# Cross-attention stage of a pre-norm decoder layer: two of four exponential tiles transposed by DMA, and row sums taken from the value product

## Chip, cores and metric

One Trainium2 chip, one core. The metric is the device time of one execution in microseconds (us), median of three runs.

## What is computed

```python
x = x + self_attention(layernorm(x))     # x: 4 rows x 2048 tokens x 512, f32
x = x + cross_attention(layernorm(x), ctx, ctx, mask)   # ctx: 4 x 128 x 512, 16 heads of 32
x = x + ffn(layernorm(x))                # s = x @ Win (64 wide); h = relu(s*W1+b1), 16 per channel;
                                         # g = sum(h*W2)+b2; out = g @ Wout
# cross attention, per head: p = exp(q.k/sqrt(32) - max); out = (p @ v) / sum(p)
```

The self-attention stage works on other axes and fills the first 848 us of the span. The change lies in the second stage, which does the cross attention and the FFN together.

## The kernel before

**Steps and slots.** The second stage goes through 8192 tokens in 16 steps j of 512 tokens, each of four tiles t of 128 tokens. Every engine has its own program order, written out by hand in its `step(j, p)`: the four slots t = 0 to 3, and then a tail. On TensorE a slot begins with `scores(t)` (q times k of all 16 heads of tile t, into four PSUM banks `sc`). The other work of a slot belongs to tiles further down the pipeline, and `ffn_out(0)` opens the step. The tail is `ffn_in(j-1)`, `norm2_T(3)`, four `queries(m)` (the q of the next step) and `prob_T(14)`, `prob_T(15)`.

**A tile's softmax.** DVE takes the maxima (`tops(t, g)`, g = four heads), ACT the exponentials (`exps(t, g)`: four instructions of 128x128, each with `accum_out`, which gives the row sum to `total`). TensorE transposes the exponentials, four heads to a PSUM bank (`prob_T(i)`, i = 4t + g, 16 a step). ACT copies each bank to f16 (`prob_hi`, into `pT[0]`), and DVE subtracts that copy from the bank (`prob_lo`, into `pT[1]`), so that high and low f16 part carry the value together. `values(t)` (48 matmuls of 128x32: 16 heads by three products of high and low parts) multiplies the tile before by v. `normalise(t)` on DVE divides by the sums, `attn_T(t)` transposes, `attn_hi`/`attn_lo` split again, and `out_proj(t)` multiplies by Wo; its split low part comes from `attn_lo(t)`. `add_attn(t)` adds the residual, `statistics(t)` takes mean and variance, and POOL's `norm2` makes the normalised tile that `norm2_T(t)`, `norm2_hi/lo` bring to `ffn_in`.

**The FFN tail.** After `ffn_in`, ACT and DVE work in turns on eight `hinges` (ACT a relu, DVE a multiply-add into `g_sb`), mixed with the splitting of q; then ACT's `gate_hi` and DVE's `gate_lo` give `gT`, which the next step's `ffn_out(0)` waits for.

**POOL** does the first normalisation (`norm(i)`), the residual plus bias (`residual(i)`) and `norm2`; the last `norm2` of a step is `norm2(j + 1, 0)`. **SP** issues all DMAs from one queue in program order: the load of the next x (`x1`), the stores, `load_ctx` (k, mask, v).

**The ring.** All PSUM results but the scores go round four banks. A hand-written order `TURNS` gives each a place; `bank(j, turn)` waits until the user four places before has been read (`taken`).

**Waits that matter below.** `scores(t)` waits for the last exponentials of the tile before, since it overwrites their banks. `exps(t, g)` waits for the transposes of the tile before, since there is one buffer `prob`.

Of the kernel before, what the change touches and what calls it, by code (L numbers as in the profile page):

```python
# [21 lines left out]
F32 = mybir.dt.float32  # L22
# [25 lines left out]
PASSES = ((0, 0), (0, 1), (1, 0))  # L48

# [54 lines left out]
def first_block(nc, x_in, ctx_in, mask_in, x1_dram, st_dram, w_in, b_in, scratch, keep):  # L104

    with ExitStack() as stack:
# [19 lines left out]
        with ExitStack() as early:  # L126
# [10 lines left out]
            vparts = sb0("vparts", [P, R, 2, D], F16)  # L137
# [11 lines left out]
        aT = [[sb(f"aT{b}_{h}", [P, DK, P], F32R) for h in range(2)] for b in range(2)]  # L149
        x = [keep["x_tile"], sb("x_tile1", [P, R, D])]  # L150
# [19 lines left out]
        total = sb("total", [P, R, H])  # L170
# [33 lines left out]
        v_trans, v_h, v_l = sem("v_trans"), sem("v_h"), sem("v_l")  # L204
        k_prod, k_masked, k_hi, k_lo = sem("k_prod"), sem("k_masked"), sem("k_hi"), sem("k_lo")
# [45 lines left out]
        def _(sp):  # L251
# [10 lines left out]
            def store_ctx():  # L262
# [366 lines left out]
        def _(act):  # L629
            def step(j, p):  # L630
# [206 lines left out]
        def _(dve):  # L837
# [334 lines left out]
def slot_turns(t):  # L1172
# [17 lines left out]
    "pT": lambda j, i: 16 * j + i + 1,  # L1190
# [23 lines left out]
def tile_at(t, lag, parity):  # L1214
# [5 lines left out]
ENDING = [(END, "pT", 14), (END, "pT", 15), (TILES, "aT", 0), (END, "x2T", 3), (TILES, "pv", 0), (TILES, "wo", 0),  # L1220
# [3 lines left out]
        if active(j, kind, i) and (j, kind, i) not in ENDING] + ENDING  # L1224
PLACE = {turn: n for n, turn in enumerate(RING)}
# [12 lines left out]
def bank_before(j, turn):  # L1238

    at = PLACE[(j, *turn)] - 4  # L1240
    if at < 0:
        return None
    step, kind, i = RING[at]
    return kind, TURNS_OVER[kind](step, i)


CROSS_SMALL = [("kt", [P, 2, DK, C], F32R), ("fillrows", [P, C], F32R), ("v_c", [C, 2, 2, D], F16),
# [4 lines left out]
def load_rows(sp, row, scratch, ahead, k_in, v_in, p):  # L1252
# [5 lines left out]
    sp.dma_start(ahead["v_c"][:, p, :, :],  # L1258
                 scratch["v"].rearrange("r c a n -> (r c) a n")[row * P:(row + 1) * P, :, :]).then_inc(v_in[p], 16)
# [13 lines left out]
def cross_block(nc, x1_dram, st_dram, scratch, w_in, b_in, out, keep):  # L1273

    with ExitStack() as stack:
# [12 lines left out]
        sb("bout_place", [P, D])  # L1288
        for name, shape, dt in CROSS_SMALL:
# [10 lines left out]
        pT = [sb(f"pT{h}", [C, H, P], F16) for h in range(2)]  # L1300
        attn = sb("attn_c", [P, D])
        aT = [sb(f"aT_c{h}", [P, DK, P], F32R) for h in range(2)]
# [3 lines left out]
        g_sb = sb("g_sb", [P, 4 * P])  # L1306
        gT = [sb(f"gT{h}", [P, 4 * P], F32R) for h in range(2)]
        ntop = sb("ntop", [P, H])
        total = sb("total_c", [P, 2, H])
        rtotal = sb("rtotal", [P, H])  # L1310
# [5 lines left out]
        ring = [stack.enter_context(nc.psum_tensor(f"ring{i}", [P, 512], F32)) for i in range(4)]  # L1316
# [5 lines left out]
        consts, k_zero = sem("c_consts"), sem("k_zero")  # L1322
# [3 lines left out]
        bn2_done, mv2_done, var2_done, rstd2_done, x2m_done, xn2_done, bf_added = (  # L1326
            sem(f"c_{n}") for n in ("bn2", "mv2", "var2", "rstd2", "x2m", "xn2", "bf_added"))
        scored, topped, exped, summed = sem("scored"), sem("topped"), sem("exped"), sem("summed")
        relu_done, hinged, g_hi, g_lo = sem("relu_done"), sem("hinged"), sem("g_hi"), sem("g_lo")
# [8 lines left out]
        def _(sp):  # L1338
# [19 lines left out]

            def step(j, p):
# [20 lines left out]
            store(TILES + 1, 1, 3)  # L1380
# [5 lines left out]
        def _(pool):  # L1386
            def step(j, p):
# [10 lines left out]
                def residual(i, j=j):  # L1398

                    wait(pool, taken["wo"], 4 * (j - 1) + i + 1)  # L1400
                    nc.gpsimd.tensor_tensor(xr[(j + 1) % 2][:, i, :], x1[:, i, :], bo[:, :], ALU.add).then_inc(res_done, 1)

# [49 lines left out]
        def _(pe):  # L1452
            def bank(j, turn):

                before = bank_before(j, turn)
                if before:
                    wait(pe, taken[before[0]], before[1])
# [14 lines left out]
            def step(j, p):  # L1472
# [40 lines left out]
                def ffn_out(t, j=j):  # L1513
                    if not active(j, "out", t):
                        return
                    cols = slice(t * P, (t + 1) * P)
# [531 lines left out]
```

## Time and profile before

| | us |
|---|---|
| median of three runs (1783.1 to 1784.54) | 1783.86 |
| the profiled execution's own time | 1784.44 |
| its span in the profile | 1782.6 |
| mean granted TensorE clock | 0.983 |
| PE, DVE, ACT, POOL busy, share of the span | 95%, 85%, 60%, 57% |
| one step in the steady state (1186.77 to 1243.76 us) | 56.99 |

PE is TensorE's matmuls, PEld its weight loads, DVE VectorE, ACT ScalarE, POOL GpSimd. Instructions of one engine overlap somewhat: the distance from one start to the next is what an instruction takes of its engine, and its own duration is a little longer.

### The profile page before, as it was taken

What the parts mean: (1) busy time and instruction counts of PE and PEld (TensorE: products, weight loads), DVE (VectorE), ACT (ScalarE), POOL (GpSimd) and SP (SyncE); (2) the same over time, 40 slices, a digit from 0 to 9 for tenths busy, and PEclk for the clock granted to TensorE, in tenths of its full rate; (3) what the DMA queues carried; (4) which work ended last, traced back from release to release, by engine and by line L of the source; (5) the groups of instructions that cost most, each with busy time, mean ns of one, the idle gap of its engine ahead of it and who ended that gap; (6) DMA issues with size and microseconds to landing.
All of it is one profiled execution on the core that took longest, in us unless ns stands there. A gap on an engine that the chain in (4) does not pass through costs nothing.

```text
span 1782.6 us, 37666 instructions
## 1 busy us (share of the span) xinstructions
PE 1685.4 (95%) x13824; PEld 1392.6 (78%) x13824; DVE 1514.8 (85%) x2089; ACT 1069.8 (60%) x3420; POOL 1017.6 (57%) x721
## 2 busy tenths in 40 slices
PE   6899999999999999997799999999999999999996
PEld 5678888888888888885677787778777787777874
DVE  6788888888888888787678898888988899888886
ACT  4434444444443334442767788777877788777884
POOL 3267766666666666695554464545654465544521
PEclk9999999999999999998799999999999999999998
DMA  5410111111111111044201112011111112011101
GB/s 210 128 42 25 47 48 48 47 47 47 47 47 47 47 47 47 2 107 79 68 8 51 62 62 63 25 62 62 63 38 43 62 62 69 19 62 62 39 20 54
DMA packets 72793, 98.75 MB, mean 55 GB/s; under 512 B 22208, under 2 KB 30528, under 8 KB 72640
## 3 DMA queue, kind: packets, MB, share of 16 engines
q1 hardware_dynamic: 72064, 96.63, 17.0%
q8 instruction: 97, 1.59, 0.4%
q14 instruction: 56, 0.46, 0.1%
q10 hardware_dynamic: 576, 0.07, 0.0%
HBM read 59.66 MB, written 37.03 MB: 54 GB/s over the span
## 4 chain that ended last, share of the span: by engine, by line
PE 28%; ACT 12%; DVE 8%; issue 4%; DVEq 0%; POOL 0%; ACTq 0%; POOLq 0%
PE ring L1464 11%; ACT prob_c L1679 10%; DVE g_sb L1794 5%; PE sc L1492 5%; PE ring L1504 3%; PE ring L1469 3%; PE ring L1549 3%; PE sc L1484 2%; PE sc L1464 1%; DVE q_first L1975 1%; ACT relu L1660 1%; DVE g_sb L1791 1%; DVE gT L1803 1%; ACT gT L1669 1%; ACT pT L1648 0%
## 5 line engine op out<-in xcount | busy, mean ns | idle before, releaser
L447 PE MATMUL qb<-wqkv,xT 128*128 128x512 f32 x2304 | 551.9, 393 | 6.1 <-DVE wqkv L1016 6.1
L447 PEld LDWEIGHTS qb<-wqkv,xT 128*128 128x128 f32 x2304 | 429.7, 189 | 93.7 <-DVE wqkv L1016 6.3
L1679 ACT ACTIVATE prob_c<-sc,ntop 128x128 f32<-128x128 f32 x1024 | 362.6, 390 | 22.1 <-DVE ntop L1821 18.7
L1410 POOL TENSOR_TENSOR rstd<-vare,half_c 128x1 f32<-128x1 f32 x64 | 35.1, 549 | 433.6 <-DVE vare L1875 433.6
L1679 ACT ACTIVATION_READ_ACCUMULATOR prob_c<-sc,ntop 128x1 f32 x1024 | 236.1, 231 | 0.0
L352 POOL TENSOR_TENSOR prod_pool<-v,prob 128x1024 f32<-128x1024 f32 x64 | 179.9, 2810 | 67.8 <-DVE prob L911 62.6
L1464 PE MATMUL ring<-wqkv,aT_c 128*128 128x512 f32 x768 | 194.5, 402 | 8.0 <-DVE aT_c L1778 7.1
L663 ACT ACTIVATE v<-qb 128x512 f32<-128x512 f32 x64 | 38.3, 598 | 259.9 <-PE qb L447 249.6
L583 PE MATMUL ob<-wout,aT 128*128 128x512 f32 x768 | 191.4, 398 | 0.8 <-DVE aT L941 0.8
L1821 DVE TENSOR_REDUCE ntop<-sc 128x4 f32<-128x512 f32 x256 | 173.3, 683 | 12.3 <-PE sc L1492 9.5
L663 ACT ACTIVATE qk<-qb 128x512 f32<-128x512 f32 x128 | 76.1, 595 | 175.8 <-PE qb L447 175.8
L1778 DVE TENSOR_TENSOR pT<-ring,pT 128x512 f16<-128x512 f32 x256 | 172.0, 682 | 8.8 <-ACT pT L1648 8.8
L1464 PEld LDWEIGHTS ring<-wqkv,aT_c 128*128 128x128 f32 x768 | 139.3, 188 | 49.4 <-DVE aT_c L1778 20.0
L1464 PE MATMUL ring<-xT_c,wqkv 128*128 128x512 f32 x720 | 172.3, 398 | 0.0
L583 PEld LDWEIGHTS ob<-wout,aT 128*128 128x128 f32 x768 | 141.5, 189 | 29.4 <-DVE aT L941 1.0
L1464 PEld LDWEIGHTS ring<-xT_c,wqkv 128*128 128x128 f32 x720 | 134.5, 188 | 31.8 <-DVE xT_c L1778 0.2
L1504 PE MATMUL ring<-ident,prob_c 128*128 128x128 f32 x1024 | 142.4, 278 | 6.3 <-ACT prob_c L1679 5.9
L1648 ACT ACTIVATE pT<-ring 128x512 f16<-128x512 f32 x256 | 141.6, 624 | 0.1
L1504 PEld LDWEIGHTS ring<-ident,prob_c 128*128 128x128 f32 x1024 | 117.6, 144 | 16.3 <-ACT prob_c L1679 9.2
L849 DVE TENSOR_TENSOR prod<-qk 128x512 f32<-128x512 f32 (+1 forms) x64 | 129.6, 2025 | 0.3
L372 POOL TENSOR_TENSOR rstd<-vare,half 128x4 f32<-128x4 f32 x16 | 16.3, 1020 | 189.0 <-DVE vare L877 189.0
L1794 DVE SCALAR_TENSOR_TENSOR g_sb<-relu,hinge,g_sb 128x512 f32<-128x512 f32 x112 | 107.0, 956 | 6.8 <-DVE g_sb L1791 0.5
(152 smaller groups left out, 3358.5 us busy)
## 6 DMA issues: line engine op xcount, KB each, us to landing
x_tile<-in_x SPq DMA_DIRECT2D x16, 1024.0 KB, 5.2
x_scratch<-xres SPq DMA_DIRECT2D x16, 1024.0 KB, 4.6
x_tile<-x_scratch SPq DMA_DIRECT2D x16, 1024.0 KB, 5.3
out<-x SPq DMA_DIRECT2D x64, 256.0 KB, 2.0
kt<-k_scratch SPq DMA_DIRECT2D x16, 512.0 KB, 3.2
v_c<-v_scratch SPq DMA_DIRECT2D x16, 256.0 KB, 3.6
raw<-in_wqkv SPq DMA_DIRECT2D x3, 1024.0 KB, 8.9
ctx<-in_ctx SPq DMA_DIRECT2D x1, 1024.0 KB, 8.3
```

The costliest lines, as they stand in the source:

```text
L352: nc.gpsimd.tensor_tensor(prod_pool[:, :, :].rearrange("p s (h d) -> p (s h) d", d=DH), v[:, s:s + 2, :].rearrange("p s (h d) -> p (s h) d ...
L447: last = nc.tensor.matmul(qb[g % 4][:, :], xT[p][a][:, k, t * P:(t + 1) * P], wqkv[b][:, k, c * D:(c + 1) * D], start=(n == 0), stop=(n == ...
L583: last = nc.tensor.matmul(ob[t % 2][:, :], aT[t % 2][a][:, k, :], wout[b][:, k, :], start=(n == 0), stop=(n == 11))
L663: nc.scalar.activation(dst, qb[g % 4][:, :], ACT.Copy, scale=SCALE if c == 0 else 1.0).then_inc(qkv_sb, 1)
L849: nc.vector.tensor_tensor(prod[:, 0:n, :], qk[:, 1, 0:n, :], qk[:, 0, t:t + 1, :].to_broadcast([P, n, D]), ALU.mult).then_inc(qk_mul, 1)
L1464: last = nc.tensor.matmul(dst, s, m, start=(n == 0), stop=(n == len(terms) - 1))
L1504: last = nc.tensor.transpose(dst[:, h * P:(h + 1) * P], prob[:, 4 * g + h, :], ident[:, :])
L1648: nc.scalar.activation(dst, ring[bank_of(j, (kind, i))][:, :], func, **kw).then_inc(hi[kind], 1)
L1679: last = nc.scalar.activation(prob[:, h, :], sc[g][:, (h % 4) * C:(h % 4 + 1) * C], ACT.Exp, bias=ntop[:, h:h + 1], accum_out=total[:, t % ...
L1778: nc.vector.tensor_tensor(dst, src, hi_part, ALU.subtract).then_inc(taken[kind], 1)
L1794: nc.vector.scalar_tensor_tensor(out=g_sb[:, :], in0=relu[:, i % 4, :], scalar=hinge[:, 2, i:i + 1], in1=g_sb[:, :], op0=ALU.mult, op1=ALU ...
L1821: nc.vector.tensor_reduce(ntop[:, 4 * g:4 * g + 4], sc[g][:, :].rearrange("p (h c) -> p h c", c=C), AX.X, ALU.max, negate=True).then_inc(t ...
```

## The change

For tiles 2 and 3 of each step the exponentials are no longer transposed on TensorE. ACT copies them from `prob` to f16 in two parts of eight heads (`part_hi`), DVE (tile 2) or POOL (tile 3) subtracts (`part_lo`), and SP issues a transposing DMA for each part, high and low (`turn`): eight DMAs of 256 KB a step. `pT` has two buffers. v gets a 33rd column of ones for each head, so that the value product gives the row sums; `accum_out` goes, `values` writes two adjoining banks, and `ring_places` gives `pv` a width of two. `values(3)` (tile 2) moves behind `norm_T(3)`, and `normalise(3)` behind `norm_lo(3)`. The pieces of the diff, in this order: SP (`turn` and the step), POOL (`part_lo` and its place), TensorE (`values` and the end of the step), ACT (`part_hi`, `exps`, the order from slot 2 on), DVE (the order from slot 2 on; its `part_lo(t, part)` is POOL's with `p_lo[t - 2]`).

```diff
+            def turn(j, t, part):
+
+                m = 2 * j + t - 2
+                heads = slice(8 * part, 8 * part + 8)
+                for h in range(2):
+                    if h == 0:
+                        wait(sp, p_hi, 2 * m + part + 1)
+                    else:
+                        wait(sp, p_lo[t - 2], 2 * j + part + 1)
+                    wait(sp, psum["pv"], 4 * j + t - 1)
+                    sp.dma_start_transpose(pT[t % 2][h][:, heads, :],
+                                           p16[h][:, heads, :].rearrange("p h c -> p (h c)")).then_inc(turned[part], 16)
...
-                if active(j - 1, "out", 3):
-                    store(j - 1, 1 - p, 3)
                 for t in range(R - 1):
                     if active(j, "out", t):
                         store(j, p, t)
+                if has(j):
+                    turn(j, 2, 0)
+                    turn(j, 2, 1)
                 if has(j, 1):
                     load_ctx(j + 1, 1 - p)
+                if active(j, "out", 3):
+                    store(j, p, 3)
+                if has(j):
+                    turn(j, 3, 0)
+                    turn(j, 3, 1)
...
+                def part_lo(part):
+                    m = 2 * j + 1
+                    heads = slice(8 * part, 8 * part + 8)
+                    wait(pool, p_hi, 2 * m + part + 1)
+                    wait(pool, turned[part], 32 * m)
+                    nc.gpsimd.tensor_tensor(p16[1][:, heads, :], prob[:, heads, :], p16[0][:, heads, :],
+                                            ALU.subtract).then_inc(p_lo[1], 1)
...
                     residual(3)
+                part_lo(0)
                 norm2(j + 1, 0)
+                part_lo(1)
...
+                    n = over - 1
+                    if n % 4 < 2:
+                        wait(pe, taken["pT"], TURNS_OVER["pT"](n // 4, 4 * (n % 4) + 3))
+                    n_dma = 2 * (n // 4) + n % 4 - 2 if n % 4 >= 2 else None
...
+                        if n_dma is not None and h % 8 == 0:
+                            wait(pe, turned[h // 8], 32 * (n_dma + 1))
+                        for i, (a, b) in enumerate(PASSES):
+                            last = nc.tensor.matmul(dst[:, head // 8, head % 8, :], pT[n % 2][a][:, h, :],
+                                                    v[:, pp, b, head, 0:DH + 1],
...
                 scores(3)
                 attn_T(3)
                 norm_T(0)
-                prob_T(10)
-                prob_T(11)
                 out_proj(3)
                 norm_T(1)
                 ffn_out(3)
-                values(3)
                 norm_T(2)
                 norm_T(3)
-                prob_T(12)
-                prob_T(13)
+                values(3)
...
-                prob_T(14)
-                prob_T(15)
...
+                def part_hi(t, part):
+
+                    m = 2 * j + t - 2
+                    heads = slice(8 * part, 8 * part + 8)
+                    wait(act, exped, 16 * j + 4 * t + 2 * part + 2)
+                    wait(act, turned[part], 32 * m)
+                    nc.scalar.activation(p16[0][:, heads, :], prob[:, heads, :], ACT.Copy).then_inc(p_hi, 1)
...
                     for h in range(4 * g, 4 * g + 4):
                         last = nc.scalar.activation(prob[:, h, :], sc[g][:, (h % 4) * C:(h % 4 + 1) * C],
-                                                    ACT.Exp, bias=ntop[:, h:h + 1],
-                                                    accum_out=total[:, t % 2, head_of(h):head_of(h) + 1])
+                                                    ACT.Exp, bias=ntop[:, h:h + 1])
...
                     exps(t, 1)
+                    if t == 2:
+                        part_hi(2, 0)
                     exps(t, 2)
                     exps(t, 3)
+                part_hi(2, 1)
+                norm2_hi(2)
+                attn_hi(3)
+                exps(3, 0)
+                norm_hi(0)
+                exps(3, 1)
+                part_hi(3, 0)
+                norm_hi(1)
+                exps(3, 2)
+                exps(3, 3)
                 norm_hi(2)
                 norm_hi(3)
+                part_hi(3, 1)
...
                     normalise(t)
+                    if t == 2:
+                        part_lo(2, 0)
                     statistics(t)
+                part_lo(2, 1)
+                norm2_lo(2)
+                tops(3, 0)
+                attn_lo(3)
+                tops(3, 1)
+                norm_lo(0)
+                tops(3, 2)
+                tops(3, 3)
+                add_attn(3)
+                norm_lo(1)
+                add_out(3)
+                statistics(3)
                 norm_lo(2)
                 norm_lo(3)
-                prob_lo(j, 12)
-                prob_lo(j, 13)
+                normalise(3)
```

The slot orders of `TURNS` follow the same edits. In the first stage `vparts` gets the layout with 34 columns a head, two small memsets fill the new ones, and its DMAs carry 136 KB instead of 128. `aT` and `gT` move into free columns of a weight tile.

## Rows read from the trace of the kernel before

**Rows 1.** Windows, slots 2, 3: length, busy PE PEld DVE ACT POOL, clock, DMA, GB/s.
```profile
1206.43:1216.34 9.91, 9.66 (x141) 8.05 (x141) 9.42 (x18) 8.73 (x39) 6.34 (x6) 1.00 0.08 29
1216.34:1227.73 11.39, 11.06 (x152) 9.35 (x152) 10.48 (x19) 10.18 (x42) 6.34 (x6) 1.00 0.52 163
```

**Rows 2.** Timeline of PE: start, length, instructions, wait before in brackets.
```profile
1196.53 0.50 PE L1484 MATMUL sc<-fillrows,ones 32*128 32x512 f32 x4 [0.64 <-ACT prob_c L1679]
...
1208.64 1.04 PE L1504 MATMUL ring<-ident,prob_c 128*128 128x128 f32 x8
...
1216.34 0.51 PE L1484 MATMUL sc<-fillrows,ones 32*128 32x512 f32 x4 [0.25 <-ACT prob_c L1679]
...
1220.28 3.04 PE L1464 MATMUL ring<-wqkv,aT_c 128*128 128x512 f32 x12
...
1227.34 0.63 PE L1504 MATMUL ring<-ident,prob_c 128*128 128x128 f32 x4 [0.26 <-ACT prob_c L1679]
...
1243.76 0.96 PE L1464 MATMUL ring<-wqkv,gT 128*128 128x512 f32 x3 [0.41 <-DVE gT L1803]
```

**Rows 3.** Timeline of ACT in slot 2: two exponentials, an accumulator read between them.
```profile
1209.40 0.36 ACT L1679 ACTIVATE prob_c<-sc,ntop 128x128 f32<-128x128 f32 x1
1209.65 0.20 ACT L1679 ACTIVATION_READ_ACCUMULATOR prob_c<-sc,ntop 128x1 f32 x1
1209.74 0.37 ACT L1679 ACTIVATE prob_c<-sc,ntop 128x128 f32<-128x128 f32 x1
```

**Rows 4.** Timeline of DVE from the end of slot 2 into slot 3.
```profile
1214.06 0.68 DVE L1821 TENSOR_REDUCE ntop<-sc 128x4 f32<-128x512 f32 x1
...
1216.80 0.69 DVE L1778 TENSOR_TENSOR x2T<-ring,x2T 128x512 fp32r<-128x512 f32 x1 [0.17 <-ACT x2T L1648]
...
1219.45 0.69 DVE L1778 TENSOR_TENSOR aT_c<-ring,aT_c 128x512 fp32r<-128x512 f32 x1
```

**Rows 5.** Groups by shape, first stage: operands in SBUF.
```profile
L930 DVE TENSOR_TENSOR prod<-prod 128x1024 f32<-128x1024 f32 x32 | 79.8, 2494 | 1.1
L849 DVE TENSOR_TENSOR prod<-qk 128x1024 f32<-128x1024 f32 x15 | 18.4, 1230 | 0.1
```

**Rows 6.** Timelines of POOL and then DVE, slot 3 and tail.
```profile
1220.57 2.55 POOL L1401 TENSOR_TENSOR xr<-x_tile,bo 128x512 f32<-128x512 f32 x2
1228.28 0.55 POOL L1410 TENSOR_TENSOR rstd<-vare,half_c 128x1 f32<-128x1 f32 x1 [5.15 <-DVE vare L1875]
...
1232.16 1.24 POOL L1392 TENSOR_TENSOR xn_c<-x_tile,st_c 128x512 f32<-128x512 f32 x1
...
1232.60 2.79 DVE L1794 SCALAR_TENSOR_TENSOR g_sb<-relu,hinge,g_sb 128x512 f32<-128x512 f32 x2
...
1239.39 1.60 DVE L1794 SCALAR_TENSOR_TENSOR g_sb<-relu,hinge,g_sb 128x512 f32<-128x512 f32 x2
```

**Rows 7.** DMA: the queue (packets, MB, share of 16 engines), and landing times.
```profile
q1 hardware_dynamic: 72064, 96.63, 17.0%
...
x_tile<-x_scratch SPq DMA_DIRECT2D x16, 1024.0 KB, 5.3
out<-x SPq DMA_DIRECT2D x64, 256.0 KB, 2.0
...
v_c<-v_scratch SPq DMA_DIRECT2D x16, 256.0 KB, 3.6
```

**Rows 8.** The ending: timeline of PE.
```profile
1728.73 0.51 PE L1484 MATMUL sc<-fillrows,ones 32*128 32x512 f32 x4 [0.26 <-ACT prob_c L1679]
...
1744.08 1.37 PE L1549 MATMUL ring<-v_c,pT 128*128 128x32 f16 x48
...
1756.80 0.65 PE L1469 MATMUL ring<-ident,xn 128*128 128x128 f32 x4 [2.94 <-DVE xn L1812]
1758.86 4.61 PE L1464 MATMUL sc<-x2T,wqkv 128*128 128x512 f32 x12 [1.41 <-DVE x2T L1778]
```

**Rows 9.** Windows: the stretch of that product, columns as in rows 1.
```profile
1758.86:1763.30 4.44, 4.44 (x12) 3.58 (x13) 2.88 (x4) 1.86 (x3) 0.00 (x0) 0.62 0.00 0
```

More of the change, by code:

```diff
@@ L1223, with ring_places @@
 RING = [(j, kind, i) for j in range(TILES) for kind, i in TURNS
-        if active(j, kind, i) and (j, kind, i) not in ENDING] + ENDING
-PLACE = {turn: n for n, turn in enumerate(RING)}
+        if (j, kind, i) not in ENDING] + ENDING
+def ring_places():
+    place, user, n = {}, {}, 0
+    for turn in RING:
+        width = 2 if turn[1] == "pv" else 1
+        if n % 4 + width > 4:
+            n += 1
+        place[turn] = n
+        for at in range(n, n + width):
+            user[at] = turn
+        n += width
+    return place, user
+PLACE, USER = ring_places()
 def bank_of(j, turn):
@@ L1235, in head_of, with banks_before @@
     return 4 * (slot % 4) + slot // 4
[L1238 to L1247, printed above, removed]
+def banks_before(j, turn):
+    first = PLACE[(j, *turn)]
+    found = []
+    for at in range(first, first + (2 if turn[0] == "pv" else 1)):
+        at -= 4
+        while at >= 0 and (at not in USER or not active(*USER[at])):
+            at -= 4
+        if at >= 0 and USER[at] not in found:
+            found.append(USER[at])
+    return [(kind, TURNS_OVER[kind](step, i)) for step, kind, i in found]
+CROSS_SMALL = [("kt", [P, 2, DK, C], F32R), ("fillrows", [P, C], F32R), ("v_c", [C, 2, 2, H, VW], F16),
                ("bo", [P, D], F32), ("bf", [P, D], F32), ("hinge", [P, 3, PAIRS], F32), ("bin", [P, 1], F32),
@@ L1305, in cross_block @@
         relu = sb("relu", [P, 4, 4 * P])
-        g_sb = sb("g_sb", [P, 4 * P])
-        gT = [sb(f"gT{h}", [P, 4 * P], F32R) for h in range(2)]
+        gT = [part[:, :, FREE_COLS + P:FREE_COLS + 2 * P] for part in keep["wqkv"]]
         ntop = sb("ntop", [P, H])
-        total = sb("total_c", [P, 2, H])
-        rtotal = sb("rtotal", [P, H])
+        rtotal = sb("rtotal", [P, 2, H // 2])
         half = sb("half_c", [P, R])
@@ L1315, in cross_block, with value_sums @@
         sc = [stack.enter_context(nc.psum_tensor(f"sc{m}", [P, 512], F32)) for m in range(4)]
-        ring = [stack.enter_context(nc.psum_tensor(f"ring{i}", [P, 512], F32)) for i in range(4)]
+        ring_all = stack.enter_context(nc.psum_tensor("ring", [P, 4, 512], F32))
+        ring = [ring_all[:, i, :] for i in range(4)]
+        def value_sums(j, t):
+            first = bank_of(j, ("pv", t))
+            return ring_all[:, first:first + 2, 0:8 * (DH + 1)].rearrange("p b (h e) -> p b h e", e=DH + 1)
         psum = {k: sem(f"psum_{k}") for k in TURNS_OVER}
@@ L1453, in bank @@
             def bank(j, turn):
-                before = bank_before(j, turn)
-                if before:
-                    wait(pe, taken[before[0]], before[1])
+                for kind, over in banks_before(j, turn):
+                    wait(pe, taken[kind], over)
                 return ring[bank_of(j, turn)]
@@ L1932, in step @@
                 statistics(0)
-                for t in (1, 2, 3):
+                for t in (1, 2):
                     norm2_lo(t - 1)
```

154 lines of the change are left out of this document (78 added, 76 removed).

## The prediction

> **What bounds the kernel now.** I read the windows by slot first, then the timelines of PE, ACT, DVE and POOL over one step, then the DMA rows and the ending. The step from 1186.77 to 1243.76 us takes 56.99 us, at full granted clock. In slot 2 PE is busy 9.66 of 9.91 us, but DVE is busy 9.42 too; in slot 3 the two have 11.06 and 10.48 of 11.39 [rows 1]. So PE sets the pace, with DVE one short instruction behind. PE's waits show where the others reach it: 0.64 us before scores(1) and 0.25 before scores(3) (scores(2) has the same wait), each for the last exponentials of the tile before, and 0.41 us before ffn_out(0) for gate_lo [rows 2]. At 95% of the whole span PE is also the busiest engine. The question is therefore not what PE loses but where DVE, which loses less and at other places, becomes the one waited for.
>
> **PE.** Eight groups of four transposes leave a step: two in slot 2, four in slot 3, two in the tail. Two groups show as 1.04 us, 0.98 from start to start [rows 2], so PE sheds 8 x 0.49 = 3.9 us a step. `values` takes 48 matmuls as before, of 33 columns instead of 32: at 1.37 us for 48 [rows 8] that is at most 1.37/32 = 0.04 us each time, and perhaps nothing; I take nothing.
>
> **ACT.** An exponential starts 0.25 us before its accumulator read, and the next exponential 0.34 us after it [rows 3]. Without the read four take 1.0 instead of 1.36 us. Eight copies out of PSUM leave a step and four `part_hi` come. A part is 128x1024: at eight times the pitch of a 128x128 exponential, 0.25 us [rows 3], at most 2.0 us each; at one start cost instead of eight nearer to half, and I take 1.0. `part_hi(2, 0)` stands between exps(2, 1) and exps(2, 2), where ACT would wait for DVE's maxima anyway. Cost nothing; if it were 2.0 us, scores(3) would come up to 0.5 us later.
>
> **Slots 0 and 1.** With shorter exponentials the waits before scores(1) and scores(2) go: -0.64 and -0.24 us. DVE also loses prob_lo 14 and 15 at the step's start. The ring needs a look, since `pv` now takes two banks. By `ring_places` a step uses 40 places, so every step has the same pattern: prob_T(5) and attn_T(2) wait for normalise(1), which ends about when PE gets there (0.1 us at most), xT 3 waits for add_attn(3), and values(3) for add_out(3). I count 0.2 us for the last.
>
> **Slot 2.** Let S2 be the start of scores(2), 1206.43 us before. tops(2, 3) starts at S2 + 7.63 [rows 4] and is done at 8.3; four exponentials later, at S2 + 9.45, scores(3) can start, against 9.91 before. PE is ready at 8.7, so it waits 0.75 us for ACT. Gain 0.46 us, not the 0.98 that PE sheds here.
>
> **Slot 3, where the gain is lost.** From the end of tops(2, 3) DVE must do: normalise(2), part_lo(2, 0), statistics(2), part_lo(2, 1), then norm2_lo(2), tops(3, 0) and attn_lo(3) at 0.6 us each. tops(2, 3), normalise(2) and statistics(2) took 1214.06 to 1216.63, when DVE fell idle for 0.17 us [rows 4]: 2.57 us, less 0.6 for the maxima, leaves 2.0. Before, four low parts of the transposed exponentials stood in the slot, of which two lay ahead of attn_lo(3). A `part_lo` is a subtraction of 128x1024 with two SBUF inputs: 1.23 us where it has SBUF to itself, 2.49 where POOL works beside it [rows 5]. The first meets an idle POOL: 1.23. The second starts together with norm2(j, 3) on POOL: I take 1.6, nearer to the low end since POOL begins with 0.55 us of tiny work. attn_lo(3) ends at S2 + 8.3 + 2.0 + 1.2 + 1.6 + 1.8 = 14.9, which is 5.45 us after scores(3). PE has scores(3), attn_T(3) and norm_T(0), 2.7 us, and then stands 2.8 us in front of out_proj(3). Before, out_proj(3) started 3.94 us after scores(3) [rows 2]. From there to ffn_in PE took 7.45 us (1220.28 to the end of slot 3 [rows 1, 2]), 1.3 of them prob_T(12) and (13) with a wait of 0.26 [rows 2]; now 6.15 and 0.2 for the ring. So ffn_in starts 5.45 + 6.35 = 11.8 us after scores(3), against 11.39: **a loss of 0.4 us** although PE sheds two us here. Bounds: both parts at 1.23 give 11.4, both at 2.49 give 13.9.
>
> **Tail.** Before, 16.03 us from ffn_in to ffn_out(0). The chain is ffn_in, eight hinges on DVE, the gates; prob_T(14) and (15) fill PE's time beside it. Dropping them alone would give nothing but 0.4 us more: PE's own tail falls to 14.6 us, the chain remains. But the chain changes. A hinge with two SBUF inputs takes 1.35 us while POOL works (2.79 for two) and 0.75 when it rests (1.60 for two) [rows 6]. norm(0) and norm(1) of the next step began on POOL at 1232.16 [rows 6] and, as four operations of up to 1.24 us, ran beside hinges 1 to 4. Now norm2(j + 1, 0), 3.9 us [rows 6], starts after statistics(3) about 11.9 us after scores(3), part_lo(1) follows at 15.8, at the rate of 2.55 us for 1024 columns [rows 6] or somewhat more with DVE against it, and so covers the first three hinges as before. Then SP: the x load of the next step stands behind turn(3, 1), whose low part waits for that part_lo. It is issued near 20 and lands 5.3 us later [rows 7], so norm(0) no longer lies beside hinges 3 and 4. They save 0.65 us: tail 15.4 us. norm_T(0) needs xn only 30 us after that. If POOL's part and norm lay on all the hinges, the tail would be 1.5 us longer than before.
>
> **The DMAs.** A part is 256 KB. Nearest rows: 2.0 us for a store and 3.6 for the v load of the same size [rows 7]; by packets, 0.17 x 16 x 1782.6 us over 72,064 is 67 ns each, and 1024 runs of 256 bytes over 16 engines give 4.3 us. I take D = 3. Last needed of tile 2 is the low half of part 1: issued at S2 + 13.1, behind two others issued at 10.4. If they run one after another, it lands at S2 + 10.4 + 3D. values(3) starts 1.2 us before ffn_in, and its second half 0.6 later: 9.45 + 11.8 - 0.6, or S2 + 20.65. So D up to 3.4 us costs nothing. Tile 3 has 11 us of room. load_ctx and store 3 wait behind them on SP, with 20 us to spare.
>
> The Trainium skill ("VectorE: DVE Perf Modes", section on the three transpose paths) speaks against the change: it gives 1309 ns for a 128x128 block through the DMA crossbar, against 390 on TensorE. If blocks of a part followed one another at that price, a part would be an estimated 10.5 us, eight of them 84 us, longer than a step. Its page "DMA: Bandwidth & Descriptors" has a rate of 261 GB/s for such transfers, about 1.0 us a part by estimate besides a fixed cost near 2 us. No row here shows either.
>
> **Sum.** -0.64 - 0.24 - 0.46 + 0.4 - 0.65 = -1.6 us a step, 55.4 instead of 57.0. Fifteen steps: -24. The last step has the first three terms, -1.3, and no queries to cover part_lo(1): values(0), 15.35 us after scores(3) before [rows 8], must wait for statistics(3) at 11, norm2 3.9, part_lo 2.55 and a DMA of 3: 20.4, or +5 us. The new layout of v in the first stage is worth less than 1 us. Together -20: 1784.4 - 20 = **1764 us**. The profiled execution stands 0.6 us above the median, no matter here.
>
> **Rivals.**
> *Late transposes (slower).* Each step waits 3D - 10.25 us in values(3). At D = 3.6 that is 0.55 us (1772), at 4.3 it is 2.65 us: 1764 + 15 x 2.65 = 1804. It decides from D = 3.9. For it: rows 7 reach from 2.0 to 4.3. Against: DMAs behind each other usually overlap, as kt, mask and v do. 0.22.
> *Block by block.* Eight blocks of a part in turn, each at the shortest landing, 2.0 us [rows 7]: 16 us a part, 128 a step. 848 + 16 x 128 + 45 = 2940 us. This is the mechanism of the skill's first figure; with that figure the estimate is 2240. 0.08.
> *DVE and POOL collide.* part_lo(2, 1) at 2.49 us, +0.9 a step: 1778; some of the hinges too, 1785. 0.08.
> *The clock falls.* After waits of 2.94 and 1.41 us twelve matmuls took 4.61 us, at a granted clock of 0.62 (between the levels of 1.2 and 2.4 GHz) [rows 8, 9], against 3.04 [rows 2]. The new wait of 2.8 us could do that to out_proj(3): +1.57 x 15, 1788. Against: PE is busy before and after. 0.08.
> *PE keeps what it sheds.* If out_proj(3) is not late, 3.9 us a step, less the ending's 5: 1731. DVE at 9.42 of 9.91 us speaks against it; halfway, 1745. 0.08.
> My forecast has 0.46, with its own range of 1754 to 1774.
>
> **From these the numbers.** The range 1742 to 1806 leaves out block by block, D above 4.3 (0.04) and the better part of the last rival (0.07). Within 0.2% (3.6 us) is about what a measurement of this kernel can't tell from no change. Faster: 0.46 + 0.08 + 0.05 of the collision + 0.04 of late transposes = 0.63. Same: 0.03 + 0.04 of the clock + 0.02 = 0.09. Slower: 0.16 + 0.04 + 0.08 = 0.28.
>
> **What would show it.** Right: a step of 55.4 us; before out_proj(3) some 2.8 us of PE waiting for DVE; before scores(3) 0.75 us for ACT; no wait in values for a DMA; the x load issued after turn(3, 1); hinges 3 and 4 near 0.75 us. Wrong: PE waits in values(3) for a DMA; transposes that land after 4 us or more; 12 matmuls of out_proj(3) above 3.1 us; a DVE part_lo above 2 us; a PE without the wait in slot 3.

## The result, and the profile after

The changed kernel takes **1805.74 us** (median of four runs, 1805.2 to 1806.49), against 1784.08 us for the kernel before in as many runs beside it: a ratio of **1.0122, 95% interval 1.0105 to 1.014**. The forecast was 1764 us, so it had the wrong sign. The range, 1742 to 1806, only just holds the time.

The page of the changed kernel first: busy times, the queue, and the row of the transposing DMAs.

```profile
span 1804.0 us, 35727 instructions
...
PE 1648.7 (91%) x13312; PEld 1355.6 (75%) x13312; DVE 1481.1 (82%) x1995; ACT 983.8 (55%) x2332; POOL 1098.3 (61%) x753
...
q1 hardware_dynamic: 207232, 130.53, 28.9%
...
pT<-p SPq DMA_TRANSPOSE x128, 3.2
```

PE fell from 95% of the span to 91%, and no other engine comes near. The mean granted clock went from 0.983 to 0.968. A transposing DMA lands 3.2 us after its issue, as assumed (3).

The second question is where in a step the time goes. This is PE's timeline over the same step as in [rows 2]: start, length, instructions, wait before in brackets.

```profile
1191.82 0.96 PE L1532 MATMUL ring<-wqkv 128*128 128x512 f32 x3 [1.45 <-DVE wqkv L1883]
...
1200.85 0.51 PE L1552 MATMUL sc<-fillrows,ones 32*128 32x512 f32 x4
...
1210.38 0.63 PE L1572 MATMUL ring<-ident,prob_c 128*128 128x128 f32 x4 [0.32 <-ACT prob_c L1749]
1210.94 0.53 PE L1552 MATMUL sc<-fillrows,ones 32*128 32x512 f32 x4
...
1220.46 0.50 PE L1552 MATMUL sc<-fillrows,ones 32*128 32x512 f32 x4 [0.72 <-ACT prob_c L1749]
1220.80 1.45 PE L1560 MATMUL sc<-kt,q_first 32*128 32x128 f32 x48
1222.18 0.66 PE L1537 MATMUL ring<-ident,attn_c 128*128 128x128 f32 x4
1222.68 0.60 PE L1537 MATMUL ring<-ident,xn_c 128*128 128x128 f32 x4
1225.49 4.61 PE L1532 MATMUL ring<-wqkv 128*128 128x512 f32 x12 [2.21 <-DVE wqkv L1858]
...
1232.59 1.36 PE L1622 MATMUL ring<-v_c,pT 128*128 128x33 f16 x48 [0.49 <-issue]
1233.80 3.05 PE L1532 MATMUL sc<-x2T,wqkv 128*128 128x512 f32 x12
...
1250.05 0.97 PE L1532 MATMUL ring<-wqkv 128*128 128x512 f32 x3 [1.53 <-DVE wqkv L1883]
```

The first and the last line are ffn_out(0) of this step and of the next, those with `sc<-fillrows,ones` are scores(1) to scores(3), that with `sc<-x2T,wqkv` is ffn_in: they cut the step into the parts of the prediction. The waits for the exponentials before scores(1) and scores(2) are gone. The twelve matmuls of out_proj(3) come after the foreseen wait, but take 4.61 us, not the 3.04 of [rows 2]. The window of that stretch, columns as in [rows 1], says why: the granted clock.

```profile
1225.49:1229.94 4.45, 4.45 (x13) 3.44 (x13) 2.43 (x4) 3.10 (x9) 4.45 (x5) 0.62 1.01 238
```

0.62 of full speed is what the same number of matmuls had in [rows 9], where 1.2 and 2.4 GHz also mix.

| part of a step, us | before | forecast | after |
|---|---|---|---|
| ffn_out(0) to scores(1) | 9.76 | 9.1 | 9.03 |
| slot 1 | 9.90 | 9.66 | 10.09 |
| slot 2 | 9.91 | 9.45 | 9.52 |
| slot 3, to ffn_in | 11.39 | 11.8 | 13.34 |
| tail, to ffn_out(0) | 16.03 | 15.4 | 16.25 |
| step | 56.99 | 55.4 | 58.23 |

The misses are +0.43, +1.54 and +0.85 us. A step is 1.24 us longer than before. Over the span: the first stage gave 0.75 us (the first scores(0) stands at 844.16 us, 844.91 before), the first two steps took it back (the first ffn_out(0) stands at 959.07, 958.79 before), from there to the last scores(3) it is 15.9 us more (785.80 for 769.94), and from the last scores(3) to the end 59.13 us (1744.87 to 1804.0) instead of 53.87: +5.3, where +5 was forecast. That agreement is luck, as told below.

The tail's miss shows on DVE (first fence) and POOL (second), with three of DVE's hinges in the kernel before (third):

```profile
1237.75 2.13 DVE L1871 TENSOR_SCALAR g_sb<-relu,hinge,b 128x512 f32<-128x512 f32 x1 [1.82 <-ACT relu L1727]
1239.99 1.61 DVE L1874 SCALAR_TENSOR_TENSOR g_sb<-relu,hinge,g_sb 128x512 f32<-128x512 f32 x2
...
1242.77 1.60 DVE L1874 SCALAR_TENSOR_TENSOR g_sb<-relu,hinge,g_sb 128x512 f32<-128x512 f32 x2
...
1247.14 1.41 DVE L1874 SCALAR_TENSOR_TENSOR g_sb<-relu,hinge,g_sb 128x512 f32<-128x512 f32 x1
```

```profile
1237.45 2.15 POOL L1467 TENSOR_TENSOR p<-prob_c,p 128x1024 f16<-128x1024 f32 x1
1246.96 1.04 POOL L1449 TENSOR_TENSOR xn_c<-x_tile,st_c 128x512 f32<-128x512 f32 x1 [7.36 <-DMA st_c<-st_scratch]
```

```profile
1231.69 0.81 DVE L1791 TENSOR_SCALAR g_sb<-relu,hinge,b 128x512 f32<-128x512 f32 x1 [1.09 <-ACT relu L1660]
...
1236.57 2.24 DVE L1794 SCALAR_TENSOR_TENSOR g_sb<-relu,hinge,g_sb 128x512 f32<-128x512 f32 x2
...
1241.56 0.74 DVE L1794 SCALAR_TENSOR_TENSOR g_sb<-relu,hinge,g_sb 128x512 f32<-128x512 f32 x1
```

The first hinge (hinge 0 in the expectations) starts 0.3 us after POOL's part_lo(1) and ends 0.28 us after it; the last, the eighth, has norm(0) beside it. Those in between take 0.8 us each.

### The profile page after: what moved, and what is told of

Read it like the earlier page. It is cut to its first block, busy times and chain, and to the rows that moved or that the text cites. A ratio compares the mean times of both kernels' runs of the same rounds, so it can differ in the third digit from the quotient of the medians.

```text
span 1804.0 us, 35727 instructions
## 1 busy us (share of the span) xinstructions
PE 1648.7 (91%) x13312; PEld 1355.6 (75%) x13312; DVE 1481.1 (82%) x1995; ACT 983.8 (55%) x2332; POOL 1098.3 (61%) x753
## 4 chain that ended last, share of the span: by engine, by line
PE 37%; DVE 9%; ACT 3%; issue 3%; POOL 0%; DMA 0%; DVEq 0%; ACTq 0%; POOLq 0%
PE ring L1532 21%; PE sc L1560 4%; PE ring L1537 3%; PE ring L1572 3%; PE sc L1532 2%; PE ring L1622 2%; DVE g_sb L1874 2%; ACT prob_c L1749 1%; DVE ntop L1901 1%; PE sc L1552 1%; DVE wqkv L1858 1%; DVE p L1916 1%; DVE x L1950 1%; ACT relu L1727 1%; DVE stats L1959 1%
## 5 line engine op out<-in xcount | busy, mean ns | idle before, releaser
L1532 PE MATMUL ring<-wqkv 128*128 128x512 f32 x960 | 273.3, 436 | 70.5 <-DVE wqkv L1858 41.8
L1749 ACT ACTIVATE prob_c<-sc,ntop 128x128 f32<-128x128 f32 x1024 | 289.3, 384 | 65.8 <-DVE ntop L1901 63.1
L1532 PEld LDWEIGHTS ring<-wqkv 128*128 128x128 f32 x960 | 189.9, 208 | 130.6 <-DVE wqkv L1858 54.4
L1477 POOL TENSOR_TENSOR rstd<-vare,half_c 128x1 f32<-128x1 f32 x64 | 50.0, 782 | 271.9 <-DVE vare L1964 271.9
L1449 POOL TENSOR_TENSOR xn_c<-x_tile,st_c 128x512 f32<-128x512 f32 x60 | 68.3, 1139 | 109.4 <-DMA st_c<-st_scratch 109.4
L404 POOL TENSOR_TENSOR xres<-x_tile,bout 128x512 f32<-128x512 f32 x64 | 109.4, 1741 | 0.1
L1727 ACT ACTIVATE relu<-sc,hinge 128x512 f32<-128x512 f32 x128 | 92.1, 775 | 29.9 <-issue 24.5
L1622 PEld LDWEIGHTS ring<-v_c,pT 128*128 128x128 f16 x3072 | 83.4, 96 | 29.8 <-DVE pT L1858 14.7
L1715 ACT ACTIVATE wqkv<-ring 128x512 fp32r<-128x512 f32 x64 | 38.3, 598 | 121.8 <-PE ring L1537 121.8
L1560 PEld LDWEIGHTS sc<-kt,q_first 32*128 32x128 f32 x3072 | 99.6, 192 | 2.6
```

The source lines that it names most:

```text
L404: last = nc.gpsimd.tensor_tensor(xres[p][:, t, :], x[p][:, t, :], bout[:, :], ALU.add)
L1532: last = nc.tensor.matmul(dst, s, m, start=(n == 0), stop=(n == len(terms) - 1))
L1560: last = nc.tensor.matmul(sc[i][:, m * C:(m + 1) * C], q[a][part, m, cols], kt[part, b, m, :], start=False, stop=done)
L1622: last = nc.tensor.matmul(dst[:, head // 8, head % 8, :], pT[n % 2][a][:, h, :], v[:, pp, b, head, 0:DH + 1], start=(i == 0), stop=(i == 2))
L1727: nc.scalar.activation(relu[:, i % 4, :], sc[number][:, :], ACT.Relu, bias=hinge[:, 1, i:i + 1], scale=hinge[:, 0, i:i + 1]).then_inc(relu ...
L1749: last = nc.scalar.activation(prob[:, h, :], sc[g][:, (h % 4) * C:(h % 4 + 1) * C], ACT.Exp, bias=ntop[:, h:h + 1])
```

## The experiments

Theory A: the wait of slot 3 lowers the clock, and that costs most of the miss. Theory B: work on POOL and DVE collides in the tail. Rivals: POOL, SP and the ring, or a price of the value product. All edits are against the changed kernel unless said. The kernel before took 1783.78 us beside the two kernels with a filled gap in slot 3, that with attn_lo(3) first and the first that takes POOL off the hinges; 1782.79 beside the two with four matmuls ahead of ffn_out(0); and 1783.68 beside the other four. The times of steps are those of one profiled execution.

### Matmuls, or transposes, in the gap

```diff
+                    if i == 0:
+                        for _ in range(8):
+                            nc.tensor.matmul(dst[:, :], wo[0][:, 0, 0:P], wo[0][:, 0, :], start=True, stop=True)
                     transpose_tile(dst, xn[:, i, :]).then_inc(psum["xT"], 1)
```

In the other kernel the loop is `for _ in range(4): transpose_tile(dst, xn[:, i, :])`. In both the real transposes overwrite the result.

> Changed kernel, plus eight matmuls of 128x512 whose results are overwritten, put before norm_T(0)'s transposes into the same PSUM bank. They add 8 x 0.24 = 1.9 us of TensorE work inside the 2.2 us in which TensorE waits for attn_lo(3). Theory A (the wait lowers the clock): the twelve matmuls of out_proj(3) after it fall from 4.6 to 3.05 us, at a granted clock of 1.0; a step loses 1.5 us, 15 of them 23 us: 1783 us, although TensorE has more to do. Rival B (DVE's chain through norm_lo(1) and add_out(3) sets the end of slot 3 anyway): out_proj(3) gets short but the time comes back as a wait before values(3); above 1800 us. Rival C (out_proj(3) is slow for another reason, such as its new operands' place): it stays at 4.6 us and the time at 1806.

> As e1, but the filler is norm_T(0)'s own four transposes done five times instead of once, 4 x 0.49 = 1.95 us more. If transposes hold the clock as matmuls do: as e1, out_proj(3) at 3.05 us and about 1783 us. If they do not: out_proj(3) stays near 4.6 us and the time near 1806.

With matmuls: 1786.63 us (1784.96 to 1794.45, 8 runs), ratio 1.0026, interval 1.0013 to 1.0039. With transposes: 1786.66 us, one run. PE's timeline with the matmuls:

```profile
1213.25 2.11 PE L1605 MATMUL ring<-wqkv 128*128 128x512 f32 x8
1215.20 0.60 PE L1537 MATMUL ring<-ident,xn_c 128*128 128x128 f32 x4
1216.15 3.02 PE L1532 MATMUL ring<-wqkv 128*128 128x512 f32 x12 [0.36 <-DVE wqkv L1862]
```

And with the transposes:

```profile
1213.33 2.35 PE L1537 MATMUL ring<-ident,xn_c 128*128 128x128 f32 x20
1216.18 2.99 PE L1532 MATMUL ring<-wqkv 128*128 128x512 f32 x12 [0.50 <-DVE wqkv L1862]
```

PE did more work and the kernel became 19 us faster: with the matmuls this step takes 56.45 us (1182.50 to 1238.95), most others 56.6 to 56.8. The wait itself was not shortened, only filled, so of the 19 us nearly all is the clock. Theory A holds. It is not the whole loss: with the gap filled the kernel is still 3 us slower than the one before.

The length of the wait alone does not decide. In the last step of the changed kernel PE stood longer in front of out_proj(3), and the clock held; there no transposes of norm_T(0) lie between attn_T(3) and the wait. Why it held wasn't followed up. The row, and the window of it:

```profile
1749.91 3.67 PE L1532 MATMUL ring<-wqkv 128*128 128x512 f32 x15 [2.66 <-DVE wqkv L1858]
```

```profile
1749.91:1753.50 3.59, 3.59 (x15) 2.74 (x15) 2.30 (x4) 3.50 (x12) 2.64 (x3) 1.00 0.50 91
```

### attn_lo(3) before the second part_lo on DVE

```diff
                     statistics(t)
-                part_lo(2, 1)
                 norm2_lo(2)
                 tops(3, 0)
                 attn_lo(3)
+                part_lo(2, 1)
```

> Changed kernel, DVE's order alone: norm2_lo(2), tops(3, 0), attn_lo(3) and only then part_lo(2, 1), which before stood first. attn_lo(3) comes 1.2 us earlier, so out_proj(3) starts about 1 us after norm_T(0) and not 2.2. Theory A: with the shorter wait the clock stays, so 1.2 + 1.5 = 2.7 us a step less, 15 steps 40 us: 1766 us. If the clock falls all the same: 1.2 us a step, 1788 us. Rival B: below 0.5 us a step, above 1798 us.

1779.08 us (1771.81 to 1786.67, 10 runs), ratio 0.997, interval 0.9955 to 0.9985: faster than both kernels, but 13 us above what was expected, with an unusual spread. PE's timeline:

```profile
1019.23 4.20 PE L1532 MATMUL ring<-wqkv 128*128 128x512 f32 x12
...
1185.10 0.96 PE L1532 MATMUL ring<-wqkv 128*128 128x512 f32 x3 [1.42 <-DVE wqkv L1883]
...
1217.62 3.08 PE L1532 MATMUL ring<-wqkv 128*128 128x512 f32 x12 [1.06 <-DVE wqkv L1858]
...
1240.80 0.96 PE L1532 MATMUL ring<-wqkv 128*128 128x512 f32 x3 [1.41 <-DVE wqkv L1883]
```

In slot 3 the wait is 1.06 us and the clock holds. This step takes 55.70 us. But of the 13 steps between 957.57 and 1689.26 us three take 58.05 or 58.06, and each of the three has twelve matmuls of 3.8 to 4.2 us soon after ffn_out(0), as at 1019.23. In front of ffn_out(0) PE waits 1.4 us for the gate, in the slow steps as in the others.

### Four matmuls in the gap of the tail

The last kernel, with this ahead of ffn_out(0)'s wait:

```diff
+                    if t == 0 and is_step(j, j) and j < TILES:
+                        early = bank(j, ("out", t))
+                        for _ in range(4):
+                            nc.tensor.matmul(early[:, :], wo[0][:, 0, 0:P], wo[0][:, 0, :], start=True, stop=True)
```

> The kernel of e3_attn_first, with four more matmuls of 128x512 (overwritten afterwards) on TensorE ahead of the wait of ffn_out(0) for gate_lo, where e3 stood 1.4 us and where some of its steps then had products at a lower granted clock. Theory (e3 fell short of its expected 1766 because of the clock after that wait): the four take about 1.0 us, leave a wait of 0.4, cost nothing, and products of over 3.2 us become few (e3: 6 or more); the spread of e3 (1771.8 to 1786.7) narrows, and the median is 1768 to 1773. Rival (the spread and the missing us of e3 come from the tail's chain on DVE and POOL, hinge 0 held by POOL, which filler can't cure): 1777 to 1781, spread as before, step at 55.7.

1773.76 us (1773.6 to 1775.29, 4 runs), ratio 0.9948, interval 0.9932 to 0.9965. The spread shrank from 15 us (10 runs) to 1.7 (4 runs), the wait from 1.41 to 0.44 us:

```profile
1234.03 1.08 PE L1587 MATMUL ring<-wqkv 128*128 128x512 f32 x4
...
1235.55 0.98 PE L1532 MATMUL ring<-wqkv 128*128 128x512 f32 x3 [0.44 <-DVE wqkv L1887]
```

One of 13 steps still takes 58.10 us, nine take 55.6 to 55.7. So most of what the kernel with attn_lo(3) first was short of, and of its spread, was the clock. The slow step begins with a late gate, and PE's timeline shows it:

```profile
1460.26 0.97 PE L1532 MATMUL ring<-wqkv 128*128 128x512 f32 x3 [1.50 <-DVE wqkv L1887]
...
1461.49 2.40 PE L1560 MATMUL sc<-kt,q_first 32*128 32x128 f32 x48
...
1466.41 4.05 PE L1532 MATMUL ring<-wqkv 128*128 128x512 f32 x12
```

The last hinge had norm(0) beside it there (1.42 us at 1457.34, against 0.74 at 1233.30, in the step of the fence before), so PE stood 1.50 us in spite of the four matmuls, and the granted clock was 0.56 in the scores after it and 0.72 in the twelve matmuls. Another late gate, with 1.20 us of waiting, had no such step behind it.

### Taking POOL off the hinges

Two kernels. In the first POOL's second part of tile 3 goes to DVE:

```diff
                 norm2(j + 1, 0)
-                part_lo(1)
...
                 normalise(3)
+                wait(dve, p_lo[1], 2 * j + 1)
+                part_lo(3, 1)
```

In the second norm(0) of the next step waits for the last hinge:

```diff
                     wait(pool, x1_in, 32 * (j + 2))
+                    wait(pool, hinged, PAIRS * (j - 1))
                     norm(0)
```

> Changed kernel, with tile 3's second part_lo moved from POOL to DVE, behind normalise(3), where DVE stood idle for 1.8 us before the first hinge. Theory D (POOL's 2.15 us part_lo(1) holds up the first hinge, 2.13 instead of 0.8 us): the first hinge back to about 0.8 us, but DVE's own part_lo of 1.2 us beside POOL's norm2 may take up to 2.5 and start it late by 0.6: 0.7 to 1.3 us a step less in the tail, 1786 to 1796 us; the ending 2 us shorter, since the DMA is issued earlier. Rival (the tail is set by TensorE's queries): no change, 1804 or more.

> Changed kernel, with one more wait on POOL: norm(0) of the next step starts only when the eighth hinge of this one is done. In the changed kernel it starts beside that hinge, which takes 1.41 instead of 0.75 us. Theory D2 (POOL's share of SBUF lengthens the tail's chain there): ffn_out(0) comes 0.67 us earlier in each step, 14 steps 9 us: 1796 us. Rival (the chain waits for something else there): no change, 1806 us.

The first: 1801.82 us (1797.98 to 1803.86, 4 runs), ratio 1.0097, interval 1.008 to 1.0114. The second: 1800.09 us (1799.38 to 1800.64, 4 runs), ratio 1.0093, interval 1.0076 to 1.0109. DVE in the first:

```profile
1235.56 1.48 DVE L1915 TENSOR_TENSOR p<-prob_c,p 128x1024 f16<-128x1024 f32 x1
1237.46 1.02 DVE L1870 TENSOR_SCALAR g_sb<-relu,hinge,b 128x512 f32<-128x512 f32 x1 [0.42 <-ACT relu L1726]
...
1244.04 2.20 DVE L1873 SCALAR_TENSOR_TENSOR g_sb<-relu,hinge,g_sb 128x512 f32<-128x512 f32 x2
```

The first hinge fell from 2.13 to 1.02 us, but SP issues the load of x at 1238.39 us (1240.96 in the changed kernel, where scores(3) stands 0.3 later), norm(0) starts at 1244.66, and falls on two hinges that took 1.60. This step is one of the better ones: 0.56 us in the tail (15.69 us, 1233.50 to 1249.19) and not the full 1.1. In most others norm(0) meets the last hinge again (1.43 us at 1304.80), and the twelve steps from 1017.40 us on take 57.96 us on average, against 58.25 in the changed kernel: 0.3 us a step. The gate on norm(0) brings the last hinge back to 0.75 us and the tail to 15.87 (1229.90 to 1245.77), the same 0.4 us in nearly every step. Theory B holds, but the two kernels are worth 4 and 6 us where the clock's part is 19.

### The column of ones alone

All four tiles' exponentials stay on TensorE; only the sums come from the product with two banks:

```diff
-                if has(j):
-                    turn(j, 2, 0)
-                    turn(j, 2, 1)
...
-                    if t == 1:
-                        prob_T(4)
-                        prob_T(5)
+                    prob_T(4 * t)
+                    prob_T(4 * t + 1)
```

(with the part_lo and part_hi left out and `TURNS` as before the change).

> One part of the change alone: sums from the column of ones and the two-bank value product, with all four tiles transposed on TensorE in the order of the kernel before. Theory E (the accumulator reads cost TensorE the waits before scores(1), (2) and (3), 1.1 us a step): these waits go, 16 steps 18 us: 1766 us. Rival F (two banks of a ring of four make TensorE wait for normalise, 0.3 us or more in each slot): half of it or all is given back, 1775 to 1795 us. In the first case the DMAs and the part copies bring the whole loss of the change; in the second a part of it.

1779.27 us (1777.97 to 1782.06, 7 runs), ratio 0.9977, interval 0.9965 to 0.9988; a step of 56.64 us (1182.39 to 1239.03), against 56.99, but six of 13 steps take 56.9 to 57.0 and the mean is 56.78. PE's waits for exponentials before `scores` are gone, and others stand in their place:

```profile
1200.07 0.63 PE L1539 MATMUL ring<-ident,prob_c 128*128 128x128 f32 x4 [0.32 <-ACT prob_c L1713]
...
1220.78 0.63 PE L1504 MATMUL ring<-ident,xn_c 128*128 128x128 f32 x4 [0.30 <-DVE x L1883]
```

The place is a `bank` of the ring both times: `pv` takes two banks now. (The profile names the exponentials for the first; the product's bank comes free with normalise(1), which ends at 1199.93.) So of the 1.1 us of [rows 2] that the shorter exponentials could free, 0.2 to 0.35 is left. The value product is not the loser: 48 matmuls of 33 columns take 1.36 us, those of 32 took 1.37 [rows 8].

### All three edits on DVE and POOL together

```diff
-                part_lo(1)
...
+                    wait(pool, hinged, PAIRS * (j - 1))
...
                 attn_lo(3)
+                part_lo(2, 1)
...
+                part_lo(3, 1)
```

> Changed kernel with three edits together: attn_lo(3) before part_lo(2, 1), tile 3's second part_lo on DVE, and norm(0) behind the eighth hinge. The first alone gave 1779 us, with steps of 55.7 us where the clock held, and a fall of the clock after the wait of 1.4 us before ffn_out(0) in some steps. The other two shorten that wait by 0.4 and 0.67 us. If they add up and the clock then holds: 1779 - 15 x 1.0 = 1764, less 3 us in the ending: 1761 us, and little spread between runs. If the shorter tail only uncovers TensorE's own work: 1770 us. If the clock falls as often as before: 1770 to 1780 us.

**1766.76 us** (1764.9 to 1771.36, 4 runs), ratio **0.991, interval 0.9892 to 0.9927**: it beats both kernels. PE, then DVE:

```profile
1211.93 3.06 PE L1532 MATMUL ring<-wqkv 128*128 128x512 f32 x12 [1.07 <-DVE wqkv L1858]
...
1217.78 1.36 PE L1622 MATMUL ring<-v_c,pT 128*128 128x33 f16 x48 [0.79 <-DVE xT_c L1858]
...
1234.86 0.96 PE L1532 MATMUL ring<-wqkv 128*128 128x512 f32 x3 [1.14 <-DVE wqkv L1883]
```

```profile
1221.03 1.31 DVE L1916 TENSOR_TENSOR p<-prob_c,p 128x1024 f16<-128x1024 f32 x1
1222.95 0.58 DVE L1871 TENSOR_SCALAR g_sb<-relu,hinge,b 128x512 f32<-128x512 f32 x1 [0.61 <-ACT relu L1727]
...
1231.66 0.75 DVE L2068 SCALAR_TENSOR_TENSOR q_first<-ring,bq,q_first 128x512 fp32r<-128x512 f32 x1 [0.53 <-ACT q_first L1715]
```

A step takes 55.43 us (1179.43 to 1234.86). That this is the forecast's 55.4 is luck: slot 1 takes 10.08 us (9.66 forecast), slot 3 10.95 (11.8), the tail 15.87 (15.4). The tail is as long as with the gate on norm(0) alone. The first hinge is short now, but further on DVE stands 0.53 us for ACT's part of q, which comes from TensorE's queries. So what the part on DVE adds in a step, beside the gate, is not shown. No twelve matmuls above 3.2 us are left between the first step and the ending. Twelve of the 13 steps to 1678 us lie between 55.0 and 55.5.

Two more kernels start from this one. The first moves prob_T(5) from slot 1 to slot 2, to free the ring; the second adds the four matmuls ahead of ffn_out(0).

```diff
-                + ([("pT", 4), ("pT", 5)] if t == 1 else []))
+                + ([("pT", 4)] if t == 1 else []))
```

> As e9, and prob_T(5) moved from the end of slot 1 into slot 2, behind attn_T(2). In the changed kernel it waits 0.32 us for normalise(1), since the value product holds its bank. Theory (that wait is lost time): 0.3 us a step, 5 us below e9. Rival (attn_T(2) then waits for the same normalise(1), or scores(3) waits longer for its exponentials): within 2 us of e9.

> The kernel of e9_attn_part_gate with the same four matmuls ahead of the wait of ffn_out(0) (1.14 us in e9). If e9 has no clock loss left in its steps, as its profile shows (products of over 3.2 us only at the start and in the ending): 1765 to 1768, no difference from e9. If the clock still falls there in other executions of it: 1763 to 1765. If the four matmuls come late and push ffn_out(0): 1770 or more.

The first is a miss: 1791.45 us (1783.33 to 1794.97, 10 runs), ratio 1.0042, interval 1.0029 to 1.0055. PE stands elsewhere:

```profile
1208.74 3.71 PE L1534 MATMUL ring<-wqkv 128*128 128x512 f32 x15 [1.14 <-DVE wqkv L1861]
```

DVE has the low part of prob_T(5) ahead of attn_lo(2) now, and it stood 0.83 us there for ACT's high part, so attn_lo(2), and with it out_proj(2), came later. Its steps take either 56.35 or 57.3 us, and what chooses between the two wasn't found.

The second: **1764.95 us** (1763.89 to 1766.94, 4 runs), ratio 0.9903, interval 0.9886 to 0.9919, not to be told from the kernel without the fill. There the steps had lost nothing to the clock, as its profile had said.

## Why the prediction failed

**The step that failed.** It is the end of "Slot 3, where the gain is lost". The wait was foreseen: out_proj(3) starts 5.03 us after scores(3) (5.45 forecast) after 2.21 us of waiting (2.8 forecast). What follows was sized at full clock, 6.35 us to ffn_in; it took 8.31. Of the 1.96 between them 1.57 are out_proj(3) itself at 0.62 of the clock, and most of the rest is the wait in values(3), 0.49 us where 0.2 was counted. The forecast had this as a rival, with the right size (+1.57 x 15, 1788) and a chance of 0.08, "against: PE is busy before and after". That reason is what the runs refute: [rows 8, 9] had shown the fall after waits of 2.94 and 1.41 us with a group of transposes between them. Filling the wait gives back 19 us, and behind a wait shortened to 1.06 us the same product takes 3.08. The rows gave no ground for so small a chance: a wait of 2.8 us was forecast, and the nearest such wait on record was followed by a lowered clock. It happened in 15 of the 16 steps; why not in the last is open.

**The tail.** Forecast -0.65 us, measured +0.22. Hinges 3 and 4 did lose their cover, as forecast: 1.60 for two instead of 2.24. POOL's part_lo(1) was said to cover "the first three hinges as before". It covers hinge 0 alone, which takes 2.13 us for 0.81, while hinges 1 and 2 take 1.61 for the 2.79 of [rows 6]: 1.32 more and 1.18 less, so this wrong step costs only 0.1 us. Hinge 0 is a `TENSOR_SCALAR` that went from 0.78 to 1.93 us on average. The rows by shape, of the kernel before and then of the changed one:

```profile
L1791 DVE TENSOR_SCALAR g_sb<-relu,hinge,b 128x512 f32<-128x512 f32 x16 | 12.5, 781 | 18.3 <-ACT relu L1660 18.3
```

```profile
L1871 DVE TENSOR_SCALAR g_sb<-relu,hinge,b 128x512 f32<-128x512 f32 x16 | 30.9, 1933 | 30.2 <-ACT relu L1727 30.2
```

The term that was missing is norm(0). x was issued at scores(3) + 20.5 us and lands 5.4 later, both as forecast, and st_c, which norm(0) needs too, about 0.6 us behind it; but norm(0) then falls on the last hinge: 0.66 us (1.41 for 0.75), most of the tail's miss. The sum asked which hinges it leaves and not which it meets.

**The other terms.** The first slot (9.03 us for 9.1) and slot 2 (9.52 for 9.45, its wait 0.72 for 0.75) were right. Slot 1 was not: prob_T(5) waits for a bank, where "0.1 us at most" was forecast. The profile calls 0.32 us idle; from start to start prob_T(4) and (5) are 0.92 us apart (1209.46 to 1210.38) instead of 0.49, and these 0.43 us are the whole miss. The two part_lo on DVE took 1.22 and 1.23 us; the second does run beside POOL, but there POOL's `rstd` is the one held, 1.48 us instead of 0.55. So that term was too large by 0.4 us, and hid as much of the clock's cost.

**The DMAs.** The two rivals against them are out. 256 KB land in 3.2 us, under the 3.9 from which it decides; values(3) of a step has no wait for a DMA but 0.49 us, called "issue", where the ring's order makes it wait for add_out(3). Only in the ending does PE wait for one, 3.12 us in the second half of values(0), and 2.30 in the best kernel. PE's timeline, of the changed kernel and then of the one before:

```profile
1764.55 0.77 PE L1622 MATMUL ring<-v_c,pT 128*128 128x33 f16 x24 [3.12 <-DMA pT<-p]
1765.17 4.57 PE L1532 MATMUL ring<-wqkv 128*128 128x512 f32 x12
```

```profile
1745.30 3.04 PE L1464 MATMUL ring<-wqkv,aT_c 128*128 128x512 f32 x12
```

The product after values(0) starts 20.30 us after scores(3) (1744.87 to 1765.17), 16.57 before (1728.73 to 1745.30): values(0) with its wait brings 3.7 us of the 5.3, and the lowered clock in that product 1.5. The forecast let all of values(0) start at 20.4 us and took nothing for the clock; its second half starts at 19.7, and the first half was done by then. On SP four of them fill up to 7.94 us, waits for the parts included; what that delays, the load of x, comes into the tail as told. The price per block in the Trainium skill ("VectorE: DVE Perf Modes", the three transpose paths: 1309 ns for 128x128) isn't what eight blocks in one DMA show here, 0.4 us a block.

**What isn't settled.** A kernel with more slack for the DMAs, or less, wasn't run, so that they cost nothing in a step rests on the trace. The single profiled executions show which steps lost the clock, but not how often over many executions. In slot 3 of the best kernel PE still waits 1.9 us a step: 1.07 for attn_lo(3), and 0.79 in front of values(3), where the profile names a low part of xT that ends at 1217.08 us, and add_out(3), for whose bank the ring's order makes it wait, ends at 1217.68.

## What to carry to other kernels

When a change takes work off TensorE but leaves it waiting for another engine, price the work behind the wait at both clocks, and look for the nearest wait of that length in the trace: here 2.2 us of waiting cost 1.57 us more in the next product, 19 us of the 22 by which the kernel became slower. Let the engine that feeds TensorE do the operand first, and its bulk work (a 1.2 us subtraction that nobody needs yet) second; where a wait must stay, idle matmuls in it are worth trying. When a transfer or a part moves on VectorE and GpSimd, list what it newly lies beside, not only what it leaves.

## What the runs showed of the hardware

- Matmuls (eight, 2.11 us) and transposes (sixteen more, 2.35 us in all) in a gap of 2.2 us kept the granted clock equally: 3.02 and 2.99 us for the twelve after it. A wait of 1.07 us in the same place left it up in every step of the best kernel. In the tail, waits of 1.4 us were followed by a fall in 3 of 13 steps of the kernel with attn_lo(3) first, waits of 1.3 to 1.7 us in none of the changed kernel's, and waits of 1.14 us in none of the best kernel's. A wait of 2.66 us in front of the last out_proj(3) left the clock at 1.00: the length of a wait alone does not tell what follows.
- A VectorE instruction with its operands in SBUF and a GpSimd instruction went one after the other where they met here, and whichever started first ran at its own pace. VectorE instructions that also read PSUM kept 0.68 to 0.69 us beside GpSimd (1223.55 to 1225.35 us in the changed kernel). A `TENSOR_SCALAR` of 0.6 us took 2.13 behind a GpSimd subtraction of 2.15, and a GpSimd operation on 128x1 took 1.48 us behind a subtraction of 1.23 on VectorE. The Trainium skill says this ("SBUF — State Buffer", two separate sides: a lock on the shared ports, held for the whole instruction); these rows agree.
- A DMA transpose of f16 from SBUF to SBUF, 256 KB, lands in 3.2 us and takes SP about 1.3 us to issue (with part_lo(3, 1) on DVE it ends at 1237.04 us, and SP is done with the last DMA at 1238.30), where a plain load of x takes 0.53.
